# Two attention layers with mixtures of experts: three banks for the exponentials' scores, 64-row stacks for queries and keys, one order for every step

## What is computed

```python
x = x + _L0_xattn_ref(_layernorm(x), ctx, ctx, Wq, bq, Wk, bk, Wv, bv, Wo, bo)   # 16 key heads
x = x + _L0_ffn_ref(_layernorm(x), w_red, wg, w1, b1, w2, b2)     # 8 experts 128-512-128, gelu, one picked
x = x + _L1_xattn_ref(_layernorm(x), ctx, wq, wk, wv, wo, gamma, beta)  # quantized, 8 key heads
x = x + _L1_ffn_ref(_layernorm(x), ...)            # 15 experts and a shared one, 128-128-128, relu, top 3
# inside an attention
scores = jnp.einsum('bhqd,bhkd->bhqk', q, k) / jnp.sqrt(d)
attn = jax.nn.softmax(scores, axis=-1)
out = jnp.einsum('bhqk,bhkd->bhqd', attn, v)
```

## Time and profile before

| | before |
|---|---|
| runs of the kernel | 285.79, 287.11, 289.53 us (median 287.11) |
| profiled execution, span from first to last instruction | 281.9 us |
| TensorE busy | 235.6 us (84%) |
| VectorE busy | 177.7 us (63%) |
| ScalarE busy | 145.3 us (52%) |
| DMA engines, mean | 58 GB/s, 16.26 MB |

### The profile page before, as it was taken

One profiled execution on the slowest core, in us unless ns is written; L12 is line 12 of the kernel. 1 busy time (PEld: TensorE's weight loads), 2 busy tenths in 40 slices (PEclk: granted clock), 3 DMA queues, 4 the chain that ended last, 5 costly groups with the idle time before them and its releaser, 6 DMA issues.

```text
span 281.9 us, 4880 instructions
## 1 busy us (share of the span) xinstructions
PE 235.6 (84%) x1685; PEld 152.1 (54%) x1700; DVE 177.7 (63%) x478; ACT 145.3 (52%) x336; POOL 54.4 (19%) x92
## 2 busy tenths in 40 slices
PE   2186345889999999999999999699699979889995
PEld 1035101344453545789988998343244424679985
DVE  5964797767656831421247137999577892589855
ACT  2026000657767686644435544366577678544542
POOL 8733982040402210100011300110000011021000
PEclk9999999799999999999999999959999999999999
DMA  6016327302270575800000110002100000000000
GB/s 158 0 60 226 150 72 162 110 4 80 74 205 22 149 190 137 215 5 2 1 0 0 58 56 2 1 0 58 56 4 0 3 0 0 3 0 0 21 1 20
DMA packets 20917, 16.26 MB, mean 58 GB/s; under 512 B 2085, under 2 KB 18989, under 8 KB 20797
## 3 DMA queue, kind: packets, MB, share of 16 engines
q1 hardware_dynamic: 20284, 15.76, 19.8%
q10 hardware_dynamic: 576, 0.13, 0.2%
q0 software_dynamic: 32, 0.07, 0.2%
HBM read 11.73 MB, written 4.19 MB: 56 GB/s over the span
## 4 chain that ended last, share of the span: by engine, by line
PE 65%; DVE 15%; ACT 7%; DMA 6%; issue 3%; SPq 2%; POOL 0%; DVEq 0%; ACTq 0%; another core or an unknown queue 0%
PE SB L1289 10%; PE OB L1226 8%; PE SA L1186 8%; DVE mx L906 7%; PE SB L1211 6%; PE OB L1302 5%; PE SB L1332 5%; PE SA L1302 5%; DMA Q<-nm 4%; PE SA L1342 4%; ACT prob L721 3%; DVE hn L871 3%; PE X L1154 2%; DVE qp L450 2%; PE X L1163 1%
## 5 line engine op out<-in xcount | busy, mean ns | idle before, releaser
L906 DVE TENSOR_REDUCE mx<-SA 128x1 bf16<-128x512 f32 x128 | 81.5, 686 | 20.0 <-PE SA L1186 15.9
L721 ACT ACTIVATE prob<-SB 128x512 f32<-128x512 f32 x128 | 69.4, 594 | 34.3 <-PE SB L1211 33.9
L1186 PE MATMUL SA<-K,Q 128*128 128x512 bf16 x113 | 41.5, 430 | 15.9 <-DVE mx L906 7.7
L1211 PE MATMUL SB<-Q,K 128*128 128x256 bf16 x256 | 41.6, 284 | 4.0 <-DMA Q<-nm 3.6
L782 ACT ACTIVATE prob<-SB,b1T 128x256 f32<-128x256 f32 x64 | 26.7, 471 | 28.5 <-PE SB L1289 28.4
L1226 PE MATMUL OB<-prob,V 128*32 128x256 f32 x512 | 39.7, 390 | 0.4 <-ACT oT L729 0.4
L1211 PEld LDWEIGHTS SB<-Q,K 128*128 128x128 bf16 x256 | 24.0, 101 | 24.9 <-ACT prob L721 6.8
L1289 PE MATMUL SB<-hT,w1s 128*128 128x256 f32 x128 | 33.3, 384 | 0.1
L1186 PEld LDWEIGHTS SA<-K,Q 128*128 128x128 bf16 x128 | 9.9, 102 | 35.6 <-DVE mx L906 23.9
L604 POOL TENSOR_SCALAR vareps<-mv 128x2 f32<-128x2 f32 x10 | 1.9, 192 | 137.2 <-DVE mv L850 137.2
L1289 PEld LDWEIGHTS SB<-hT,w1s 128*128 128x128 f32 x128 | 22.3, 190 | 3.6 <-ACT prob L782 0.7
(11 more groups left out here) (210 smaller groups left out, 282.4 us busy)
## 6 DMA issues: line engine op xcount, KB each, us to landing
w1s<-in_L_ffn_w_dram SPq DMA_DIRECT2D x8, 256.0 KB, 3.7
w2s<-in_L_ffn_w_dram SPq DMA_DIRECT2D x8, 256.0 KB, 4.4
K<-in_L_ffn_eW_dram SPq DMA_DIRECT2D x2, 960.0 KB, 6.5
K<-k_dram SPq DMA_DIRECT2D x8, 192.0 KB
Q<-q_dram SPq DMA_DIRECT2D x8, 192.0 KB
k_dram<-kp SPq DMA_DIRECT2D x2, 384.0 KB, 2.8
q_dram<-qp SPq DMA_DIRECT2D x4, 192.0 KB, 2.1
K<-k_dram SPq DMA_DIRECT2D x2, 384.0 KB
```

The source lines that it names most:

```text
L721: act.activation(prob[:, g % 2, i, 2 * u:2 * u + 2, :].rearrange("p k q -> p (k q)"), SB[u][:, :], ACT.Exp).then_inc(s_exp, 1)
L906: dve.tensor_reduce(mx[:, g % 2, r, i:i + 1], SA[SCORE_BANK[n]][:, :], AX, ALU.max).then_inc(s_sa_max, 1)
L1186: pe.matmul(SA[SCORE_BANK[u]][:, :], Q[n][:, b, s, r * P:(r + 1) * P], K[n][:, b, key_group(n, s), :], start=True, stop=True).then_inc(s_s ...
L1211: last = pe.matmul(SB[u][:, k * NQ:(k + 1) * NQ], K[n][:, b, key_group(n, s), kt * P:(kt + 1) * P], Q[n][:, b, s, :], start=True, stop=True)
```

## The change

The tables, the stacks and the banks are all changed:
- PSUM: SB has three banks instead of two, in rotation over the exponentials' matmul pairs. X has one bank of its own, and X1 is SB's third bank: steps between a layer's first and last exponentials use X0 alone. The prologue's transposes and layer 0's value projections use SA, SB and OB instead.
- Stacks: partition 8e+j holds row j (of eight) of feature e; rows 0 to 5 are the six part products, row 6 the shift (and the ones in K), row 7 is zero. A half of 64 rows is one head's stack, and each matmul contracts over its 64 rows alone; heads of a pair lie in the two halves. Q shrinks from 16 to 8 slots. The fills are zeros, and the ones of K's row 6 come by DMA (keys_ones).
- DRAM: each of the three parts is written once, when it is ready (three waits in turn), and each of the six rows is read by a DMA of its own. Layer 0's first queries are read from ScalarE's queue.
- kproj and qproj: ScalarE writes the first bf16 part straight from PSUM, VectorE subtracts from PSUM; the factor of the queries is in the weights.
- Exponentials: a step is one key half of a pair of heads, not one head; values of the first key half start when its exponentials are done. max_rows sends two DMAs, on one semaphore for even groups and one for odd.
- Order: scores, maxima and values stand step by step in the tables. Scores of groups 0 and 1 are issued before the first exponentials, together with the projections of batch 1 and the turned, quantized context. Work is moved between ScalarE and VectorE (ON_SCALAR), layer 1's expert weights have memory of their own, V has 9 columns per head, and the load of layer 1's weights w1n moves to the start.

```diff
-K_PART = (0, 1, 2, 0, 1, 0)
-Q_PART = (0, 0, 0, 1, 1, 2)
-SHIFT_ROW = 8 * len(K_PART)
-K_PARTS = ((2, 1), (1, 1))
+K_PART = (0, 0, 0, 1, 1, 2)
+Q_PART = (0, 1, 2, 0, 1, 0)
+SHIFT_ROW = 6
+STACK = 64
+VW = DH + 1
+K_PARTS = ((1, 1), (1, 1))
...
+    (3, 0): [('scores', 5, 0), ('values', 2, 0), ('max_rows', 4)],
+    (3, 1): [('scores', 5, 1), ('values', 2, 1)],
...
-        Q = [sb(f"Q{n}", [P, B, H, NQ], BF16) for n in range(2)]
+        Q = [sb(f"Q{n}", [P, B, 8, NQ], BF16) for n in range(2)]
-        SB = [stack.enter_context(nc.psum_tensor(f"SB{n}", [P, 512], F32)) for n in range(2)]
+        SB = [stack.enter_context(nc.psum_tensor(f"SB{n}", [P, 512], F32)) for n in range(3)]
...
-        X = [stack.enter_context(nc.psum_tensor(f"X{n}", [P, 512], F32)) for n in range(2)]
+        X = [stack.enter_context(nc.psum_tensor("X0", [P, 512], F32)), SB[2]]
...
+        def read_stack(engine, dst, row_parts, dram, written, slots, done):
+
+            for part in range(3):
+                engine.wait_ge(written[part], 16)
+                for row in (j for j, p in enumerate(row_parts) if p == part):
+                    engine.dma_start(dst[row:P:8, slots].rearrange("e s c -> e (s c)"),
+                                     dram[part, :, slots].rearrange("e s c -> e (s c)")).then_inc(done, 16)
...
+                    for part in range(3):
+                        sp.wait_ge(s_qp[n][b], part + 1)
+                        write_part(qp[:, part_buffer(step), :, :], part, q_dram[n][b], s_qwr[n][b])
...
+                    for a in range(2):
+                        row = 64 * a + SHIFT_ROW
+                        sp.dma_start(Q[n][row:row + 1, b, 2 * g:2 * g + 2, :],
+                                     nm[2 * a:2 * a + 2, step[1] % 2, :]).then_inc(s_shift[step[1] % 2], 16)
...
+                    for a in range(2):
...
-                        pe.matmul(SA[SCORE_BANK[u]][:, :], Q[n][:, b, s, r * P:(r + 1) * P], K[n][:, b, key_group(n, s), :],
+                        rows = slice(64 * a, 64 * a + STACK)
+                        pe.matmul(SA[SCORE_BANK[u]][:, :], Q[n][rows, b, p, r * P:(r + 1) * P], K[n][rows, b, key_group(n, p), :],
...
-                        if m >= 2:
-                            pe.wait_ge(s_exp, m - 1)
+                        if m >= 3:
+                            pe.wait_ge(s_exp, m - 2)
...
+                    if kt % 2 == 0:
+                        pe.wait_ge(s_exp, 8 * gg + 2 * kt + 4)
```

1110 lines of the change are left out of this document (647 added, 463 removed).

## The result

The changed kernel runs in 276.93 us (median of 4 runs, 275.91 to 280.18), the kernel before in 286.45 beside it (283.01 to 289.53). The ratio is 0.970, with an interval of 0.961 to 0.979: faster, by 3% and not by 8%. A second set of runs gave 277.19.

A forecast was written before the change was run, and what follows sets the result against it. TensorE was taken to bound both attentions and experts 0, waits the prologue, a mixture experts 1. Stages 42 + 51.6 + 66.7 + 4 + 55 + 38.9 = 258.2, plus 5.2, gave 263.4 us; range 246 to 279.

The forecast's parts named there:

- Prologue, 42 us: Stage up to the first exponentials: 42 us (38 to 49) instead of 49.3, with first exponentials at 41 to 43.
- the CAST's wait, 5.42 less the 0.6, so 4.8: Prologue, ahead of the first scores: a CAST's wait beside fills goes away, taking 4.8 us off 21.5.
- 23 x 1.35 = 31.1, and 7.2 us: Attention 0: 23 steps with scores at 1.35 us, plus 7.2 for projections, turns and splits, make 38.3 us.
- Rival 1: Attentions: row halves don't run side by side, the third bank brings nothing, steps stay 1.54 us; 269 us, chance 0.22.
- the third bank by itself removes no wait: Steady attention steps: the third bank alone gains nothing, as TensorE never waits for ScalarE in steps of 1.54 us.
- The nine late steps, 1.25 each: Attention 0's steps without scores: nine at 1.25 us make 11.3; a tail of 2 us follows.
- 2 us more waits for the shift's DMA: Attention 0's high end of 58 us: steps of 1.54 us and 2 us more of these waits.
- Experts 0 and transition, 70.7: Experts 0 stays at 66.7 us, as matmuls are the same and TensorE is 98% busy; transition stays at 4.
- Attention 1, 55 us: Layer 1's attention: 55 us (50 to 59), from 53.8 plus 1.2 for the low clock at its start.
- I leave 2, hence 40.5: Attention 1's 23 steps: VectorE's 38.5 us of work plus 2 for TensorE's wait for batch 1's queries.
- Rival 3: Attentions: the clock stays at 0.50 in more steps, each 1.5 us longer; 300 us at 25 steps, chance 0.06.
- The 5.2 us around the span: Whole kernel: the median of runs lies 5.2 us above the profiled span, so span 258.2 becomes 263.4.

The follow-up runs named there:

- f1_fills_back: Against a1, the zero fills of layer 0's K and Q go back from VectorE to GpSimd; 274.0 us.
- c1: The changed kernel with matmuls over all 128 rows and two banks instead of three for the exponentials; 279.74 us, ratio 0.979 to the kernel before.
- a4: The changed kernel with scores and exponentials matmuls contracting over all 128 rows instead of 64-row halves; 276.99 us, ratio 0.977 to the kernel before.
- a1: a1_stacks_later: the changed kernel with two reads of key stacks issued behind the shifts of groups 1 and 7; 271.46 us, ratio 0.957 to the kernel before.
- c2: Against a1, layer 1's maxima read only 256 of the 512 keys of each row; 271.71 us, ratio 0.948 to the kernel before.
- d2: Against a1, the links of the chain to batch 1's queries (statistics, norm, turn, projection) are issued earlier; 272.81 us.
- d1: Against a1, layer 1's second query stack is read from batch 0's parts, right behind the first stack; 273.54 us.
- c3_max9_later: Against a1, the turn of group 9's maxima stands behind layer 1's first exponentials instead of ahead; 273.12 us, ratio 0.953 to the kernel before.

## Why the prediction was wrong

The direction and its main mechanism were right, the size was not: 276.9 us against 263.4, inside the stated range, but with two fifths of the forecast gain. By the steps of the prediction:

- **Prologue, 42 us: right, 42.7, in part by luck.** Scores at 25 to 28 came at 26.7, csq ended at 40.4 (38.5 to 41 forecast), its turns stood right behind, and exponentials came at 42.7. But the term "the CAST's wait, 5.42 less the 0.6, so 4.8" did not come: the CAST still took 3.47 us beside the fills, where it takes 0.41 without them, and the keys' splits stood behind it. Other work that ended sooner made up for it, such as the first hn at 9.9 us and not at 11.6. The argument that the fills on VectorE bring the gain was weak: f1_fills_back lost 0.5 to 2 us, not 7.
- **"23 x 1.35 = 31.1, and 7.2 us", 38.3 until the last scores: right, 38.1 and 40.3.** Rival 1 (row halves don't run side by side) fell: exponentials take 0.23 us. But its other half, "the third bank by itself removes no wait: in rows 2 TensorE never waits for ScalarE", was the wrong reading. It was read from regular steps of 1.54 us, and for these it holds: they are 1.54 with two banks too (c1). What it missed are the steps of the new order in which nothing else stands between exponentials, 0.45 us apart in a4 and 1.1 in c1, and the short steps that half rows bring, where two banks cost 8 us.
- **"The nine late steps, 1.25 each" and "a tail of 2 us", 13.3: the step that failed in attention 0.** It measured 20.5 us (19.8 in the second set), and 15.5 with the two stacks moved. The diff says that each of the six rows is read by a DMA of its own, and its tables have a stack's read ahead of group 7's shift. The working counted the bytes of those reads and never their issues on SyncE: six of 0.75 us, where a stack had been two or four issues. "2 us more waits for the shift's DMA" was the high end; the waits were 2.72 and 3.99 (0.87 and 3.47 in the second set) and what the clock added behind them.
- **Experts 0 and transition, 70.7: 72.7.** The step "nothing changes" missed that the clock could fall there: it is 0.50 from 171.3 on, 5 us ahead of attention 1, where before had 1.00 until 182.8. With the clock at 1.00 the stage took 71.5 (a1), and with full rows 70.9. Of layer 1's first scores, 14 matmuls stood there before and 16 now.
- **Attention 1, 55 us: the other step that failed, 62.4.** VectorE's 38.5 us of work were right (38.17). That the work sets the stretch was wrong: "I leave 2, hence 40.5" took one known wait of 1.98 us and assumed the rest gap-free. The stretch took 45.4 us with the same work, and with 12 us of that work gone (c2) 45.1. The first 20 us, up to batch 1's queries, are as long as before the change; over all kernels they were 17.1 to 21.6, and the shortest are those with the chain issued sooner (d2) or with full rows. The earlier trace rows have that wait at 201.35, 19.3 us behind the first exponentials at 182.0; a sum that kept those 19.3 us as one block would have come nearer. What sets this block stays open. Not the DMA of batch 1's queries alone (d1), and not VectorE's maxima alone (c2); the written order around step (9, 0), the clock and the maxima together are what the runs leave.
- **Rival 3, the clock: half right.** The low clock came, for 24 us instead of 6 in layer 1, behind 3 us in which TensorE was busy for 1.9 (for 0.0 ahead of the fall at 92.8). Its price, "1.5 us more a step", did not: the changed kernel's attention 1 is 1.2 us longer than a4's at full rows and nearly full clock. What it does cost is not isolated: raising it from 0.79 to 0.92 by added matmuls brought nothing, and holding it by full rows brought 3.0 to 4.7 us where the maxima or the queries were out of the way.
- **The 5.2 us around the span: mis-sized.** In each run of the changed kernel, time less span is 2.0 to 2.1 us (277.63 and 275.6, 275.91 and 273.9), so the forecast span stands for a time of 260.3. The 5.2 was mostly the distance of one profiled execution of before to the median of its runs.

The step that failed, in one sentence: the forecast added up both attentions as steps times a length, and left out six DMA issues ahead of an urgent one in attention 0 (shown by moving them) and the irregular start of attention 1 (its cause open). a1_stacks_later has the lowest median of the kernels here that leave nothing out: 271.46 us, 4.3% under the kernel before on its chip and 2% under the changed one; c3_max9_later has 273.12, and the lower ratio, 0.953.
